# Keeping five lo units a block in DRAM for the second layer, and nine units instead of seven in seven products

## The reference

```python
# layer 0
deg = adj.sum(axis=1) + 1e-5
out = (adj / deg) @ x @ W_neigh.T + b_neigh + x @ W_self.T + b_self
x1 = layernorm(x + relu(out))
# layer 1, d = rowsum(adj) ** -0.5
out = (d[:, None] * adj * d[None, :]) @ x1 @ W + b
x2 = layernorm(x1 + relu(out))
```

## Time and profile before

| | |
|---|---|
| median of 3 runs | 778.12 us (777.93 to 778.42) |
| profiled execution, own time | 777.39 us |
| its span | 775.7 us |
| TensorE busy | 767.4 us, 99% |
| VectorE busy | 706.7 us, 91% |
| ScalarE busy | 425.3 us, 55% |
| DMA | 161.08 MB, mean 208 GB/s |
| granted TensorE clock | 0.999 of full speed |

### The profile page before, as it was taken

The page is one execution under the profiler, slowest core; times in us unless marked ns, Lnnn a source line. Parts: engine busy times, 40 slices in busy tenths (PEclk is TensorE's granted clock), DMA queues, the critical chain, the costliest instruction groups (busy, mean ns, idle before and its releaser), DMA issues.

```text
span 775.7 us, 12551 instructions
## 1 busy us (share of the span) xinstructions
PE 767.4 (99%) x4106; PEld 661.3 (85%) x4106; DVE 706.7 (91%) x1193; ACT 425.3 (55%) x590; POOL 2.5 (0%) x14
## 2 busy tenths in 40 slices
PE   9999999999999999999999999999999999999996
PEld 6888888888888888888888789899998989999886
DVE  6999999999899899998979999898989989898754
ACT  5654645646345464454554655665565566656552
POOL 0000000000000000000000000000000000000000
PEclk9999999999999999999999999999999999999999
DMA  7965574755647557374573756657565665746741
GB/s 301 353 233 193 198 257 155 245 185 199 239 144 243 189 178 255 137 268 167 187 257 136 243 173 213 214 192 243 170 225 199 215 217 172 261 162 228 259 143 55
DMA packets 54205, 161.08 MB, mean 208 GB/s; under 512 B 5024, under 2 KB 18080, under 8 KB 54176
## 3 DMA queue, kind: packets, MB, share of 16 engines
q1 hardware_dynamic: 45680, 151.54, 57.0%
q10 hardware_dynamic: 8352, 9.05, 3.6%
q0 software_dynamic: 144, 0.13, 0.1%
HBM read 152.31 MB, written 8.39 MB: 207 GB/s over the span
## 4 chain that ended last, share of the span: by engine, by line
PE 94%; DVE 4%; ACT 1%; issue 0%; DVEq 0%; ACTq 0%
PE ps_main L1087 69%; PE ps_epi L966 7%; PE ps_epi L1034 6%; PE ps_main L1025 4%; PE ps_main L1034 2%; PE ps_epi L1025 2%; DVE lo L569 2%; PE ps_main L1109 1%; PE ps_main L966 1%; PE ps_main L1062 1%; PE ps_main L1047 1%; DVE acc L721 1%; DVE xs L569 0%; DVE tt L625 0%; DVE tt L641 0%
## 5 line engine op out<-in xcount | busy, mean ns | idle before, releaser
L361 ACT ACTIVATE hi<-raw 128x1024 fp32r<-128x1024 f32 x254 | 256.0, 1018 | 147.7 <-PE ps_main L1087 103.4
L569 DVE TENSOR_TENSOR lo<-raw,hi 128x1024 fp32r<-128x1024 f32 x254 | 297.8, 1175 | 26.9 <-ACT hi L361 26.8
L1087 PE MATMUL ps_main<-hi,xs 128*128 128x512 f32 x1120 | 279.0, 391 | 0.4 <-DVE xs L683 0.4
L1087 PEld LDWEIGHTS ps_main<-hi,xs 128*128 128x128 f32 x1120 | 207.5, 188 | 42.4 <-DVE xs L683 0.9
L1087 PE MATMUL ps_main<-lo,xs 128*128 128x512 f32 x560 | 149.7, 389 | 0.0
L856 DVE TENSOR_TENSOR acc<-acc,raw 128x1024 f32<-128x1024 f32 x112 | 136.5, 1219 | 0.0
L1087 PE MATMUL ps_main<-hi,zs 128*128 128x512 f32 x544 | 135.4, 391 | 0.0
L1087 PEld LDWEIGHTS ps_main<-lo,xs 128*128 128x128 f32 x560 | 105.2, 188 | 21.8
L1087 PEld LDWEIGHTS ps_main<-hi,zs 128*128 128x128 f32 x544 | 100.0, 188 | 19.2
L361 ACT ACTIVATE xs<-acc 128x1024 fp32r<-128x1024 f32 (+1 forms) x47 | 49.3, 1048 | 64.0 <-DVE acc L753 51.6
L1087 PE MATMUL ps_main<-lo,zs 128*128 128x512 f32 x272 | 72.7, 389 | 0.0
(11 more groups left out here) (157 smaller groups left out, 787.1 us busy)
## 6 DMA issues: line engine op xcount, KB each, us to landing
raw<-adj_t SPq DMA_DIRECT2D x256, 512.0 KB, 3.3
res<-x_nat SPq DMA_DIRECT2D x11, 512.0 KB, 5.3
xt_sb<-xt SPq DMA_DIRECT2D x8, 512.0 KB, 5.4
x_scratch<-tt ACTq DMA_DIRECT2D x8, 512.0 KB, 4.3
res<-x_scratch SPq DMA_DIRECT2D x8, 512.0 KB, 4.7
out<-tt ACTq DMA_DIRECT2D x7, 512.0 KB, 5.0
tt<-x_nat SPq DMA_DIRECT2D x3, 512.0 KB, 4.5
acc<-x_nat ACTq DMA_DIRECT2D x1, 512.0 KB, 5.0
```

Source lines behind the costliest of these rows:

```text
L361: return act.activation(dst, src, ACT.Copy)
L569: return dve.tensor_tensor(dst, src, hi_part.bitcast(f32), ALU.subtract)
L1087: last = pe.matmul(ps[:, f, :], stationary(layer, part, jt, f), mov[:, slot(u), cols], start=(jt == 0 and i == 0), stop=(jt == JT - 1 and ...
```

## The change

Five units a block have their `lo` written from SBUF to a DRAM scratch in layer 0 (blocks 0 to 6) and read from there in layer 1, where VectorE leaves their split out and only advances the counter with a memset of one column. In block 0 they are units 4, 6, 8, 10, 11, elsewhere 0, 3, 4, 8, 11. `SU` grows from seven to nine units. The third place of the ring of split sums moves to `wn` and `ws`, which are free by then. `T_UNITS`, where weight sums are split, goes from (5, 8, 11, 14) to (2, 4, 6, 9, 11). `lead` says at which unit the sums for v are made, and whether before or after the present unit's `s_lo`.

```diff
-SU = (1, 5, 7, 9, 11, 12, 13)
+SU = (1, 2, 5, 6, 7, 9, 10, 12, 13)
 NS = len(SU)
-SUMS_AT = tuple(max(u - 2, 0) for u in SU)
 SRING = 3
+KEPT_FIRST = (4, 6, 8, 10, 11)
+KEPT = (0, 3, 4, 8, 11)
+NK = len(KEPT)
 T_AT = XC + FH
-T_UNITS = tuple(range(5, 5 + 3 * ((NS + 1) // 2), 3))
+T_UNITS = (2, 4, 6, 9, 11)
...
+        lo_dram = nc.dram_tensor("lo_scratch", [NB, NK, P, UW], f32, kind="Internal").ap()
...
+        def kept(b):
+
+            if is_first(b):
+                return KEPT_FIRST
+            return () if isinstance(b, int) else KEPT
...
+        def lead(v):
+
+            return v - 1 if v - 1 in SU and v - 2 not in range(1, NU) else max(v - 2, 0)
...
         def s_part(part, u):
 
-            at = S_AT + SU.index(u) % SRING * 4 + part * 2
+            s = SU.index(u) % SRING
+            if s == SRING - 1:
+                return (wn, ws)[part][:, :, :, :].rearrange("p a k f -> p (a k f)")
+            at = S_AT + s * 4 + part * 2
...
                     sp.dma_start(raw[:, slot(u), :], adj_in[b, u]).then_inc(raw_full[slot(u)], 16)
+                    if layer == 0 and u - RING in kept(b):
+                        sp.dma_start(lo_dram[b, kept(b).index(u - RING)], lo[:, slot(u), :].bitcast(f32)).then_inc(lo_stored[slot(u)], 16)
+                    if layer == 1 and u - RING + 1 in kept(b):
+                        v = u - RING + 1
+                        if is_first(b) and v == KEPT_FIRST[0]:
...
+                                    sp.wait_ge(lo_stored[i], stored * 16)
+                        sp.wait_ge(h_ready, g0 + (v + 1))
+                        sp.dma_start(lo[:, slot(v), :].bitcast(f32), lo_dram[b, kept(b).index(v)]).then_inc(lo_full[slot(v)], 16)
...
-                        split_lo(lo[:, slot(u), cols], raw[:, slot(u), cols], hi[:, slot(u), cols]).then_inc(l_ready, 1)
+                        if layer == 0 and u - RING in kept(b):
+                            dve.wait_ge(lo_stored[slot(u)], kept_count(b, u - RING))
+                        if layer == 1 and u in kept(b):
+                            dve.memset(marks[:, 2:3], 0.0).then_inc(l_ready, 1)
+                        else:
+                            split_lo(lo[:, slot(u), cols], raw[:, slot(u), cols], hi[:, slot(u), cols]).then_inc(l_ready, 1)
                     place(u, 1)
                     if by_seven(layer, b):
+                        ahead = [v for v in SU if lead(v) == u]
+                        slot_taken = ahead and len([v for v in SU if u <= v < ahead[0]]) == 2
+                        if ahead and not slot_taken:
+                            s_sums(b, parity, ahead[0])
                         if u in SU:
                             s_lo(b, parity, u)
-                        if u in SUMS_AT:
-                            s_sums(b, parity, SU[SUMS_AT.index(u)])
+                        if ahead and slot_taken:
+                            s_sums(b, parity, ahead[0])
...
-                        if i == 2:
+                        if i == 2 and layer == 1 and u in kept(b):
+                            pe.wait_ge(lo_full[slot(u)], kept_count(b, u))
+                        elif i == 2:
                             pe.wait_ge(l_ready, g0 + (u + 1))
```

More of the change, by code:

```diff
@@ L130, in build @@
         tt_stored = sem("tt_stored")
+        lo_stored = [sem(f"lo_stored{s}") for s in range(RING)]
+        lo_full = [sem(f"lo_full{s}") for s in range(RING)]
         ones_set = sem("ones_set")
@@ L194, in by_seven, with kept_count, same_slot @@
             return layer == 1 and not isinstance(b, int)
+        def kept(b):
+            if is_first(b):
+                return KEPT_FIRST
+            return () if isinstance(b, int) else KEPT
+        def kept_count(b, u):
+            def same_slot(units):
+                return [v for v in units if slot(v) == slot(u)]
+            at = same_slot(kept(b)).index(u) + 1
+            if is_first(b):
+                return at * 16
+            per_block = len(same_slot(KEPT))
+            return (b * per_block + (len(same_slot(KEPT_FIRST)) - per_block + at)) * 16
+        def lead(v):
+            return v - 1 if v - 1 in SU and v - 2 not in range(1, NU) else max(v - 2, 0)
         def tile_sums(layer, e, parity, t):
@@ L303, in one_block @@
                     sp.dma_start(raw[:, slot(u), :], adj_in[b, u]).then_inc(raw_full[slot(u)], 16)
+                    if layer == 0 and u - RING in kept(b):
[3 more added lines that the diff above has]
+                        if is_first(b) and v == KEPT_FIRST[0]:
+                            for i in range(RING):
+                                stored = sum(slot(w) == i for w in KEPT_FIRST + (NB - 2) * KEPT)
+                                if stored:
+                                    sp.wait_ge(lo_stored[i], stored * 16)
+                        sp.wait_ge(h_ready, g0 + (v + 1))
+                        sp.dma_start(lo[:, slot(v), :].bitcast(f32), lo_dram[b, kept(b).index(v)]).then_inc(lo_full[slot(v)], 16)
                     if layer == 0:
@@ L857, in one_block @@
                     place(u, 2)
-                    if by_seven(layer, b) and u in SUMS_AT:
-                        s_last_sum(b, parity, SU[SUMS_AT.index(u)])
+                    if by_seven(layer, b) and ahead:
+                        s_last_sum(b, parity, ahead[0])
                     if epi is None and u == NU - 1:
```

## The result

| | before | after |
|---|---|---|
| median of the runs, us | 778.09 (777.23 to 778.42, 10 runs) | 780.0 (779.25 to 780.43, 10 runs) |
| ratio to before, 95% interval | | 1.0027 (1.0019 to 1.0035) |
| profiled execution, us | 777.39 | 780.43 |
| its span, us | 775.7 | 778.7 |

The forecast was 775.8 with a range of 774.9 to 778.1: wrong in sign, and outside the range. The ten runs of before include the three given above, and their median is 0.03 lower. The profiled execution after is the slowest of its ten and the one before is 0.7 under its median, so the span is 3.0 us longer while the medians differ by 1.9. The granted clock is 0.999 of full speed in both.

The account below looks back on a forecast made before the run. TensorE, busy 767.4 of 775.7 us, was taken as the bound. From the profiled 777.39, -2.5 (conversions) - 0.4 (z) + 0.6 (stores) = -2.3 gives 775.1, forecast as 775.8 for the median; range 774.9 to 778.1.

Parts of the forecast that it names:

- TensorE 12 x 0.21: Second layer, six middle blocks: two more units each in seven products, 0.21 us saved per unit, 2.5 us less.
- The wait for z: Second layer's first block: TensorE's 0.44 us wait at 442.80 for z from VectorE goes.
- VectorE's loop: Second layer: nmr round to nmr takes some 45.2 us a block against TensorE's 44.71, losing 0.5 a block; no stall.
- The lead at block 1: Second layer: hi of unit 0 ends 6.9 us before TensorE needs it; following lead about 6.4, the last 4.4.
- The need of 2.5 us: Second layer's middle blocks: lead required so that s_lo of unit 10, the tightest place, is in time; cover 1.9 us.
- rival C: Second layer: VectorE's loop takes over, 2.8 us lost and z's wait stays; 779.0, no change; chance 0.10.
- The first block's stores: First layer's first block: stores of units 4 and 6 delay VectorE's lo of unit 10; TensorE loses 0.6 us.
- Later stores (units 8, 10, 11): First layer's first block: these come when the DMA engines have room, so no loss was counted for them.
- rival B: First layer's first block: stores report late, loss 1.6 us, giving 776.8; chance 0.17.
- The loads: Second layer: loads of kept lo have 6.2 us or more and land inside that; price 0.
- D: First layer's first block: all five stores delay VectorE in full, loss 5.7 us, slower at 780.9; chance 0.08.

Follow-up runs that it names:

- e3: Changed kernel without any stores or loads of kept lo, or waits for either; 774.7 us, ratio 0.9956.
- e7: e4 with only units 8 and 10 kept in the first block; 775.26 us, ratio 0.9963.
- e9: e4 with only units 8, 10 and 11 kept in the first block; 776.31 us, ratio 0.9974.
- e5: e4 with the first block's five stores reading a never-changing tile, so VectorE waits for none of them; 777.24 us, ratio 0.9988.
- e6: e4 with only units 4, 6 and 8 kept in the first block; 776.38 us, ratio 0.9980.
- e4: Changed kernel with kept-lo loads one unit earlier in SP's queue and waiting for TensorE's slot release, not ScalarE's hi; 778.44 us, ratio 1.0002.
- e10: Changed kernel with kept-lo loads waiting for TensorE's slot release instead of hi, place in the queue unchanged; 778.8 us, ratio 1.0013.
- e1: Changed kernel without the five stores of the first layer's first block and the waits on them; 776.7 us, ratio 0.9979.
- e8: Nine units in seven products but no unit kept: no stores, no loads, all lo split by VectorE; 801.65 us, ratio 1.0300.

## Why the prediction was wrong

Three steps failed, all of them prices of a transfer: the first block's stores of units 4 and 6, put at 0.6 us; its later stores, put at nothing; and the loads, put at nothing.

**TensorE 12 x 0.21: right.** 454.59 to 457.10 for the new unit 2; blocks of 44.70 to 44.72 us where nothing is late; e3 gives 3.4 for this and z together, against 2.9.

**The wait for z: gone as forecast, and worth more.** TensorE runs through it at 446.43 without a gap. Of the 3.3 us by which the second layer is shorter in seven traces, 2.5 are the conversions, which leaves 0.7 to 0.8 here. I took the idle time in the bracket, 0.44, where start to start was the measure.

**VectorE's loop: right in price, too good in lead.** 45.21 against 45.2 a block. Nmr of block 0 is at 436.35, or 433.0 without the first layer's 3.4, against 432.3. The lead at block 1 is 6.4 (445.43 to 451.87), near the 6.9 forecast. But at block 2 it is 4.7 (491.9 to 496.57), not 6.4, and at block 6 it is 3.4, not 4.4. The first step costs 1.8 us and not 0.5, and that stood in the prediction's own numbers: before the change the lead falls from 5.5 to 3.7 there. It falls from 6.5 to 4.8 in e7 as well, where ScalarE waits for no transfer at this place, so the raw of 9.2 us behind nmr of block 0 isn't the cause. The need of 2.5 us was right: in e9, whose leads at blocks 5 and 6 are 2.2 and 2.4, TensorE waits 0.30 and 0.03 us for s_lo in unit 10. So rival C did not happen in the changed kernel, whose 3.4 is over 2.5, but the cover is 0.9 us and not 1.9.

**The first block's stores: this step failed.** I forecast lo of unit 10 at 34.5 with a DMA as its releaser, and it came at 35.25 so; st_lo should end at 43.4 and ended at 43.9; the loss there was 1.2 instead of 0.6. That the sign came true is luck, since the mechanism behind it wasn't at work: the wait for the store of unit 6 was the last to end by 0.27 us only, and e5, which has no such wait, loses as much. What delays VectorE is raw: I let one store push raw of unit 10 by 1.4, and the raws of units 8, 9 and 10 were 1.9 to 2.1 late. Part of the difference can be seen. A price of 1.36 us for a store assumes that the engines stay full; in the trace the share fell to 0.85 from 20 to 24 us, which is 0.6 us of all engines more. The six traces with the store of unit 4 have 0.75 to 0.90 in this stretch, the six without it 0.96 to 1.02. Why the engines idle there stays open.

The larger part I missed: "Later stores (units 8, 10, 11) come when the engines have room" was read from 36 to 40 us of the kernel before, share 0.80. From 40 to 48 us there was even more room, 0.57 and 0.69. But I never summed it. The three shares leave 0.94 x 4.0 = 3.8 us of all engines between 36 and 48 us, and three stores at 1.36 want 4.1. They fill the room by themselves, without what the first two push back: e9, which lacks those two, has shares of 1.02 and 0.98 from 40 to 48 us and loses 1.1 to 1.4 us at the start of block 1. With all five stores it is 1.4 to 2.5, so what is left for a backlog from the first ones is 1.2 at most. e6, without the stores of units 10 and 11, loses nothing there.

The Trainium skill (DMA: Bandwidth & Descriptors, Anatomy of one DMA), which describes the path of transfers issued by GpSimd, says that the semaphore fires only after the last byte is confirmed. These stores go over SyncE's queue; unit 11's took 6.3 us and the raw issued beside it 5.4, which agrees in direction, but e5 shows that the wait for the semaphore is the smaller share. That speaks against rival B's mechanism too, though its 1.6 is near the 1.2.

**The loads: this step failed too.** "Price: 0; even 4.3, the slower of the two landings of rows 9, is inside" took the landing time of a DMA share of 0.60 for a kernel that runs at 0.79. Loads of kept lo took 4.5 us in the median, up to 6.6 in the middle blocks and 7.3 in the first one, and the 6.2 us that I said they had was 5.0 at block 6. I had named the sign that would refute it, a wait for loaded lo anywhere, and four are there; together they cost 3.0 us in the profile. Which event lets the load go I had read, but not questioned: e4 and e10 change only when the load is issued, and the gaps go.

**Rivals.** The sign was D's, with 0.08, though not by its mechanism: the stores cost 3.3 and not 5.7, and the loads brought the rest.

## What to carry to other kernels

A transfer's landing time is a price at a load: take it from a stretch as busy as the changed kernel will be, and take slack after each neighbour's delay, not before. Where transfers are to go into a gap of the DMA engines, add up all of them against the idle time of all stretches. Where a kernel begins with full DMA engines, keep optional stores out of that stretch; here three stores of 35, with their loads, cost 3.2 us (e4 against e7). And let an issue wait for the event that truly frees its buffer, not for a later one that implies it: that single wait was worth 3.0 us in the profiles of the second layer and 1.2 in the medians (e10).

## What the hardware showed that I had not expected

- The rate at full share is not one number. At 24 to 28 and 28 to 32 us it is 404 GB/s, at 44 to 48 us 257 at a share of 0.97. In that last stretch the transfer of the biases on GpSimd's queue is under way, 144 small packets which take 23.4% of the engines for 0.13 MB (queue, packets, MB, share):

```profile
q1 hardware_dynamic: 246, 0.90, 73.5%
q0 software_dynamic: 144, 0.13, 23.4%
```

  A packet of it has 0.9 KB and takes 0.234 x 16 x 4.0 / 144 = 0.10 us of an engine; one of the others has 3.7 KB and takes 0.735 x 64 / 246 = 0.19. The same transfer was issued at 36.92 before and at 41.56 now, and so fell on the time of unit 15's raw. It isn't enough by itself: in e6 it is issued at 41.44, and nothing is lost at the start of block 1. Nor is it the whole of the low rate: the other queue's packets were slower too, 0.19 us for 3.7 KB where the same stretch before has 0.686 x 64 / 278 = 0.16 for 3.6 KB, and this part I can't assign.
- With the DMA share of a middle block at 0.79 and not 0.60, raw lands in 4.2 us in the median where it took 3.3 (445 to 715 us), at the longest in 7.4 where it was 4.7, and one in the layer's first block, issued at 433.40, took 9.2. The tail grows more than the median, and it is the tail that meets the slack.
- With no first-block stores at all, e1, e3 and e8 have the second block's epilogue product at 62.47, 63.02 and 62.85, with before at 62.25; the four traces with all five stores and their waits have it from 65.51 to 66.63. The start of the kernel varies by some 1 us between executions, and single profiles can't settle less than that. From the second layer's first block on, traces of the same order agree within 0.1 us.
